# Two result tables for the last two experts, values before powers, and the down products moved inside the next step

## The reference

```
xn  = layernorm(x)
out = x + xn + attention(layernorm(xn) * gamma + beta) @ Wout + moe(xn)
```

```
logits = xn @ Wg.T;  top 2 experts, gates = softmax of the two logits
slot   = running count of the expert in (token, choice) order; kept if slot < 640
h      = rows[slot] @ W1[e];  y = (gelu(h[:, :256]) * h[:, 256:]) @ W2[e]
out[token] += gate * y[slot]    for each kept choice
```

## Time and profile before

| | us |
|---|---|
| median of 3 runs (lowest, highest) | 143.83 (143.49, 144.63) |
| the profiled execution: its own time | 143.37 |
| the profiled execution: span of the records | 141.6 |
| TensorE busy in the span | 108.6 (77%) |
| VectorE busy | 93.5 (66%) |
| ScalarE busy | 68.8 (49%) |
| GpSimd busy | 75.1 (53%) |

### The profile page before, as it was taken

How to read it: one execution, slowest core, us unless ns; L and a number is a source line. 1 busy time by engine, 2 the same in 40 slices (tenths; PEclk the granted TensorE clock), 3 DMA queues, 4 the chain that set the end, 5 groups by cost and what they waited for, 6 DMA issues and landing times.

```text
span 141.6 us, 2294 instructions
## 1 busy us (share of the span) xinstructions
PE 108.6 (77%) x705; PEld 97.6 (69%) x705; DVE 93.5 (66%) x299; ACT 68.8 (49%) x164; POOL 75.1 (53%) x92
## 2 busy tenths in 40 slices
PE   0039999999888884898399999999999988965000
PEld 0029769788777763786298999999999987655000
DVE  0699787696576867897337587897757330463991
ACT  0478773346558751323536666767766644410000
POOL 7700707777787787770000277877877777730000
PEclk9999999999999999999959999999999999999755
DMA  3999999999511111114990011111111111696487
GB/s 98 247 329 287 284 370 326 354 347 300 163 42 59 39 64 54 44 59 108 316 283 8 0 56 37 56 58 39 56 58 58 39 56 56 191 306 187 145 237 219
DMA packets 31980, 21.35 MB, mean 151 GB/s; under 512 B 2224, under 2 KB 29872, under 8 KB 31968
## 3 DMA queue, kind: packets, MB, share of 16 engines
q1 hardware_dynamic: 29104, 16.41, 41.3%
q0 software_dynamic: 2144, 4.53, 9.5%
q10 hardware_dynamic: 720, 0.27, 0.8%
HBM read 10.04 MB, written 11.15 MB: 150 GB/s over the span
## 4 chain that ended last, share of the span: by engine, by line
PE 35%; POOL 22%; DVE 13%; issue 11%; DMA 11%; ACT 2%; SPq 1%; POOLq 1%; DVEq 0%; ACTq 0%
POOL y_rows L447 20%; PE bank_h L935 5%; DMA y_last<-rows,target_i 5%; PE bank_h L937 4%; PE bank_h L936 4%; DMA qT<-y_last 3%; PE bank_x L1105 3%; PE bank_y L1047 3%; DMA xs<-in_x 3%; PE bank_x L1016 3%; PE bank_y L956 2%; PE bank_a L956 2%; POOL y_last L447 2%; DVE pre L763 2%; DVE stats L632 2%
## 5 line engine op out<-in xcount | busy, mean ns | idle before, releaser
L447 POOL DMA_INDIRECT y_rows<-rows,target_i x30 | 30.0, 1000 | 25.6 <-ACT rows L588 17.1
L434 POOL DMA_INDIRECT x_slots<-xa,slot_i x32 | 32.6, 1019 | 14.3 <-issue 9.4
L901 DVE TENSOR_TENSOR hid<-gelu,bank_h 128x384 f32<-128x384 f32 (+2 forms) x32 | 16.3, 510 | 19.2 <-ACT gelu L605 19.1
L1157 PE MATMUL bank_y<-w_sb,hid 128*128 128x128 f32 x172 | 21.9, 276 | 2.3 <-issue 2.3
L1157 PEld LDWEIGHTS bank_y<-w_sb,hid 128*128 128x128 f32 x172 | 21.0, 191 | 2.8 <-issue 2.7
L935 PE MATMUL bank_h<-xg_hi,w_lo 128*128 128x384 f32 (+1 forms) x56 | 20.1, 359 | 1.4 <-DVE xg_lo L852 1.2
L605 ACT ACTIVATE gelu<-bank_h 128x384 f32<-128x384 f32 (+2 forms) x32 | 14.7, 459 | 12.0 <-PE bank_h L937 11.2
L937 PE MATMUL bank_h<-xg_hi,w_hi 128*128 128x384 f32 (+1 forms) x56 | 18.0, 321 | 0.0
L936 PE MATMUL bank_h<-xg_lo,w_hi 128*128 128x384 f32 (+1 forms) x56 | 17.9, 320 | 0.0
L588 ACT ACTIVATE rows<-bank_y,gate_slot 128x128 f32<-128x128 f32 x35 | 10.6, 366 | 10.7 <-PE bank_y L1157 10.7
L935 PEld LDWEIGHTS bank_h<-xg_hi,w_lo 128*128 128x128 f32 x56 | 11.1, 197 | 2.0 <-DVE xg_lo L852 1.6
(11 more groups left out here) (156 smaller groups left out, 241.0 us busy)
## 6 DMA issues: line engine op xcount, KB each, us to landing
x_slots<-vacant SPq DMA_DIRECT2D x7, 340.0 KB, 6.7
rows<-x_slots SPq DMA_DIRECT2D x7, 340.0 KB, 5.7
w_raw<-in_w SPq DMA_DIRECT2D x4, 512.0 KB, 7.3
y_rows<-zeros SPq DMA_DIRECT2D x2, 1024.0 KB, 12.2
expo<-y_rows SPq DMA_DIRECT2D x8, 256.0 KB, 7.3
xs<-in_x SPq DMA_DIRECT2D x4, 256.0 KB, 4.5
y_last<-zeros SPq DMA_DIRECT2D x1, 1024.0 KB, 10.9
qT<-y_last SPq DMA_DIRECT2D x4, 256.0 KB, 3.8
```

Source lines behind the costliest of these rows:

```text
L434: nc.gpsimd.indirect_dma_start(x_slots, bass.IndirectOffsetOnAxis(ap=slot_i[:, k, t:t + 1], axis=0), xa[:, t, :], None,).then_inc(rows_out ...
L447: nc.gpsimd.indirect_dma_start(y_rows if r < R - 1 else y_last, bass.IndirectOffsetOnAxis(ap=target_i[:, n:n + 1], axis=0), rows[:, n, 0:D ...
L901: nc.vector.tensor_tensor(hid[s % 2][:, c, 0:cols], gelu[i % 2][:, 0:cols], bank_h[2 * c + 1][:, 0:cols], ALU.mult).then_inc(hid_ready, 1)
L1157: ins = nc.tensor.matmul(bank_y[:, j * D:(j + 1) * D], hid[s % 2][:, c, j * P:(j + 1) * P], w2_sb[:, e, c, :], start=(c == 0), stop=(c == ...
```

## The change

- Experts 6 and 7 (the last two, `LAST = 2`) get a table each, `y_last[0]` and `y_last[1]`; `y_rows` holds experts 1 to 5. SyncE fills one table more with zeros, waits for 25 scatters before it reads `y_rows`, then for the five of each last table before it reads that one (four transfers each).
- The order of the additions at the end changes: the first choice's four are behind step 14, the dense addition of step 14 and the second choice's four behind step 15, then the four of `y_last[0]`, three of `y_last[1]`, the dense addition of step 15 and the last one.
- `down(s-1)` is issued between the two halves of step s, behind the transposes. `evacuate(s-1)` comes before the gelu of the second half. `y_evac` is raised for each tile, and GpSimd waits tile by tile.
- ScalarE scales the values of a pair of tiles before it takes the pair's power.
- The state of batch 0 is computed by VectorE within the pair loop (at pair 6), that of batch 1 behind the loop; the two states accumulate in two banks.
- In the layer norm VectorE normalises group 1 before the statistics of group 2, and ScalarE copies the first transposes before the third root.
- GpSimd issues one gather of x before the scatters, of which nothing reads the result.

```
@@ note_sum / VectorE, order of the additions
+SUMS_IN_STEP: (14, 1): (("choice", 0),), (15, 1): (("dense", 14), ("choice", 1))
...
+    for g in range(G): note_sum(("last", 0, g), ...)
+    for g in range(G):
+        if g == G - 1:
+            note_dense(S - 1)
+        note_sum(("last", 1, g), ...)
@@ SyncE
             for i in range(2):
-                sp.wait_ge(y_stored[i], 16 * ST * len(range(i, R - 1, 2)))
+                sp.wait_ge(y_stored[i], 16 * ST * len(range(i, R - LAST, 2)))
...
-            sp.wait_ge(y_last_stored, 16 * ST)
+            for i in range(LAST):
+                sp.wait_ge(y_last_stored[i], 16 * ST)
+                for g in range(G):
+                    sp.dma_start(fetched_last[i][:, g * GROUP:(g + 1) * GROUP, :],
+                                 y_last_tiles[i][:, g * GROUP:(g + 1) * GROUP, :]).then_inc(last_in[i][g], 16)
@@ GpSimd
+            nc.gpsimd.indirect_dma_start(
+                unused_rows[:, :], None, x.rearrange("b l d -> (b l) d"),
+                bass.IndirectOffsetOnAxis(ap=partition[:, 0:1], axis=0),
+            ).then_inc(unused_in, 16)
...
-                for i, (j0, nj) in enumerate(PARTS):
-                    pool.wait_ge(y_evac, len(PARTS) * r + i + 1)
-                    for n in range(r * ST + j0, r * ST + j0 + nj):
+                for n in range(r * ST, (r + 1) * ST):
+                    pool.wait_ge(y_evac, n + 1)
@@ ScalarE
             for u in range(U):
+                act.wait_ge(pre_ready, 2 * u + 1)
+                scaled_values(2 * u)
                 act.wait_ge(pre_ready, 2 * u + 2)
+                scaled_values(2 * u + 1)
                 nc.scalar.activation(expo[...], pre[...], ACT.Exp, ...).then_inc(exp_ready, 1)
-                scaled_values(2 * u)
-                scaled_values(2 * u + 1)
...
                         split_rows(s + 1)
-                if s >= 1 and s != first_dense:
-                    evacuate(s - 1)
+                    if c == 0 and s >= 1 and s != first_dense:
+                        evacuate(s - 1)
@@ VectorE
+                if u == STATE_AT:
+                    state_of(0)
             elu(U - 1)
+            state_of(1)
@@ TensorE, up(s)
                     if c == 1 and s + 1 < S and steps[s + 1][3] is not None:
                         transpose_slots(s + 1)
+                    if c == 1 and s >= 1 and s != first_dense:
+                        down(s - 1)
...
                 up(s)
-                if s >= 1 and s != first_dense:
-                    down(s - 1)
```

More of the change, by code:

```diff
@@ L24 @@
 KV_LAG = 4
+STATE_AT = 6
 RESULTS_AT = 2
@@ L30 @@
 LOW_IN_STEP = {(0, 1): 2, (2, 1): 3, (4, 1): 4, (6, 1): 5, (8, 1): 6, (10, 1): 7}
[L31 to L32 removed]
+SUMS_IN_STEP = {(1, 1): (("first", 0),), (2, 1): (("first", 1),), (3, 1): (("first", 2),), (4, 1): (("first", 3),),
+                (5, 1): (("early", 0),), (7, 1): (("early", 1),),
+                (14, 1): (("choice", 0),), (15, 1): (("dense", 14), ("choice", 1))}
 DROPPED = 16384.0
 PARTS = ((0, 3), (3, 2))
+LAST = 2
 TOKEN, RANKS, GATES, ROW = 128, 129, 131, 136
@@ L85, in moe_attention_block, with note_dense @@
             note_sum((kind, u), (2 * u, 2 * u + 1))
+    def note_dense(s):
+        for j in range(GROUP):
+            note_sum(("step", s), (steps[s][1] + j,))
     for s in range(S):
         for c in range(FC):
-            if (s, c) in SUMS_IN_STEP:
-                kind, i = SUMS_IN_STEP[s, c]
+            for kind, i in SUMS_IN_STEP.get((s, c), ()):
                 if kind == "first":
                     note_sum((kind, i), tuple(range(i * GROUP, (i + 1) * GROUP)))
-                else:
+                elif kind == "early":
                     for j in range(GROUP):
                         note_sum((kind, i), (all_token_steps[i][1] + j,))
[L95 to L102, removed]
-    for g in range(G):
-        note_sum(("last", g), tuple(range(g * GROUP, (g + 1) * GROUP)))
+                elif kind == "dense":
+                    note_dense(i)
+                else:
+                    for g in range(G):
+                        note_sum((kind, i, g), tuple(range(g * GROUP, (g + 1) * GROUP)))
+    for g in range(G):
+        note_sum(("last", 0, g), tuple(range(g * GROUP, (g + 1) * GROUP)))
+    for g in range(G):
+        if g == G - 1:
+            note_dense(S - 1)
+        note_sum(("last", 1, g), tuple(range(g * GROUP, (g + 1) * GROUP)))
     def earlier_sum(index, tiles):
@@ L917, in _ @@
                             add_early(n)
-                if s >= 1:
-                    add_dense(s - 1)
-            add_dense(S - 1)
-            for k in range(TOP_K):
-                for g in range(G):
-                    add_rows(("choice", k, g), g, fetched_in[k][g], fetched[:, k, :, :])
-            for g in range(G):
-                add_rows(("last", g), g, last_in[g], fetched_last)
+                        elif kind == "dense":
+                            add_dense(n)
+                        else:
+                            for g in range(G):
+                                add_rows(("choice", n, g), g, fetched_in[n][g], fetched[:, n, :, :])
+            for g in range(G):
+                add_rows(("last", 0, g), g, last_in[0][g], fetched_last[0])
+            for g in range(G):
+                if g == G - 1:
+                    add_dense(S - 1)
+                add_rows(("last", 1, g), g, last_in[1][g], fetched_last[1])
         @block.tensor
```

81 lines of the change are left out of this document (42 added, 39 removed).

## The result

| | before | with the change |
|---|---|---|
| median (12 runs each, side by side) | 143.65 us | 145.0 us |
| lowest, highest | 143.37, 145.91 | 143.65, 147.05 |
| ratio, 95% interval | | 1.0089 (1.0048 to 1.0131) |
| a second comparison on another chip | 145.26 us | 145.44 us, ratio 1.0142 (0.9997 to 1.0286) |

Medians are of all runs, ratios and intervals only of those within 1.5% of their kernel's fastest, so the two can differ. The changed kernel is about 1.3 us slower; 144.8 was forecast. The profiled execution of the changed kernel has a span of 145.3 us, 3.7 more than before. So the traces are compared within, from the first up product of step 2 on. From there to the end of the last addition both profiles of the changed kernel agree within 0.02 us.

What follows compares the result with a forecast made beforehand. TensorE and GpSimd together were taken to bound the expert steps, with a tie of reads and VectorE's additions at the end. Front 0 plus end +1.0, stalls included, on 143.83 gave 144.8 us, range 142.2 to 146.0.

Steps and rivals of the forecast that it cites:

- The total: Whole kernel: +1.0 us, 144.8 by the median, own range 144.2 to 145.6, chance 0.5.
- The front: Values, states, layer norm and gather ahead of the steps: together 0, between -0.5 and +0.4 us.
- Its own signs of being wrong: Among them a first step over 0.5 us away from 70.8, or a second window with a granted clock near 0.5.
- Rival 4: TensorE's clock falls at one of the new stalls, costing about 1.7 us: 146.5 us, chance 0.07.
- The first scatter: GpSimd's first result scatter starts 1.3 us earlier, near 79.0; waits at each expert's first tile use up the lead.
- The stall: TensorE waits for `hid` before `down` behind three-tile halves: 0.38 us five times, 0.6 in step 13, 2.5 us in all.
- The four rows that I added up: Half's end, gelu, `hid` and handover on the way to `down`: 1.43 us, against 1.05 us of other TensorE work.
- The end: VectorE's unbroken 9.5 us of additions behind step 15 ends at 139.4, against 138.40: +1.0 us, with the reads hidden.
- Rival 1: The stall in the steps does not come, TensorE keeps 6.32 us an expert: 142.2 to 142.5 us, chance 0.25.
- The queues: Last scatter beside the reads: served in turns by packet, it would land some 4 us sooner than the 7.00 us measured.

Runs made afterwards that it cites:

- run 8: The change with the down products inside the next step in odd steps only, behind both halves in the others: 143.81 us, 0.999 of the kernel before.
- run 7: The change with the down products inside in step 1 only, and the additions at the end placed earlier: 141.22 us, 0.985 of the kernel before.
- run 5: The change with the down products inside in step 1 and the even steps, behind both halves in odd steps 3 to 13: 144.01 us, 1.002 of before.
- run 6: The change without the four additions of `y_last[0]`, whose scatters and reads stay: 143.46 us, 0.996 of the kernel before.
- run 4: The change with the down products inside in step 1 only, behind both halves in all other steps: 142.22 us, 0.988 of the kernel before.
- run 3: The change with its front undone (value and power order, states, layer norm order, gather): 144.56 us, 1.012 of the kernel before.

## Why the prediction was right, point by point

- **The total.** Forecast +1.0 us, measured +1.3, inside the forecast's own range. The mechanism, a loss in the steps that is larger than the gain at the end, is what the traces show. That the total came so close is in part luck: at the last addition +1.70 were measured for +1.0, and the 0.5 us saved behind it are in no term of the sum, which took the 3.2 us behind it as they were.
- **The front: 0 (-0.5 to +0.4).** Right where it can be read: 6.30 for 6.25 us around the states, and no difference in time when all of it is undone. The start of step 2 itself (80.80 and 79.40 for 78.30) is off by more than the range, but in profiles whose code is the same up to there it lies between 77.22 and 80.80.
- **Its own signs of being wrong.** Two of them came: step 0 started at 72.67 and 71.45 and not within 0.5 us of 70.8, and a second window with the clock at 0.50 was there. By the profiles of the same code neither belongs to the steps that the sum is about; the prediction had no measure of how far the front moves by itself. Rival 4's price of 1.7 us for a low stretch like the one before was too high as well: with it steps 0 and 1 take 7.32 us in run 8, without it 6.35 in run 7.
- **The first scatter, 1.3 us sooner.** Right: 2.01 to 0.70 us behind the start of step 2. Its last one came at 46.65 for 46.4 forecast. But the way there was wrong: I expected a wait at each expert's first tile, and GpSimd waits hardly at all (0.5 us over the usual 0.30 in all). Its lead goes into scatters that take longer, 1.30 to 1.44 us in place of 0.97, one in each of five experts; from first to last it takes 45.95 us, where 34 x 1.27 are 43.2. So the last scatter came where it was forecast by luck. Each of the five long ones starts 0.09 to 0.23 us behind the start of a `w_lo` of VectorE (the first at 85.33, `w_lo` at 85.24). The group of twelve starts near them too, but other kernels speak for `w_lo`: in the kernel before the one scatter that starts so (88.38, `w_lo` at 88.24) takes 1.38, and in run 5 one does (83.65, `w_lo` at 83.58) and takes 1.45, while the group of twelve starts only at 84.59. No run tried it by itself.
- **The stall, 5 x 0.38 + 0.6 = 2.5 us: the size of one was right (0.37 measured, 0.46 in step 13), the sum was too small, 3.03.** Even the one size is right by two errors that cancel. `hid` ends at 85.32 and the group starts at 85.38, 0.06 us behind it and not 0.15; and the first half takes 0.72 us (84.05 to 84.77) and not 0.80. Four experts lose 0.42 to 0.46 us each, the last one, with step 13, 0.71. In these, the group of eight takes 0.85 for 0.81 and the group of twelve, after a wait, 1.36 for 1.26. The expert with step 7 loses 0.57 in another way: no stall on `hid`, but 0.49 us of waiting for `xg_lo`, where before there were 0.25.
- **What causes it: this step named the wrong edit.** I wrote that the group of twelve stalls because it was moved ahead of the second half. Runs 5 and 8 show otherwise: without its move the stall and the whole loss stay (3.00 of 3.03 us), with it the stall goes and 1.41 us of loss stay for the other reasons read off in run 8. What counts for the stall is the group of eight. The four rows that I added up gave the right wait only because the group of eight is missing from "until then TensorE has only the two-tile half and three transposes". I had put it inside the even step and never asked what it had covered. And the same `hid` was not "late by nothing" before: it was 0.44 us early.
- **The end: 139.4 for 138.40.** From step 14 to the last addition's end 18.6 us were forecast, 18.77 measured; the unbroken row of 9.5 us is 133.03 to 142.60, 9.57. That the reads are hidden was right, and run 6 shows by how little.
- **Where the rest comes from.** The end is not at its best either: run 5, in which `down(14)` comes behind the last half of step 15, needs 60.52 - 43.00 = 17.52 us from step 14 on, 1.25 less than the change. With the group inside, the last `hid` ends 9.29 us behind the start of step 14 and not 7.95, and VectorE's row hangs on it. The prediction had this group (1.7 in the sum) but didn't price its alternative.
- **Rival 1 (no stall, 142.2 to 142.5).** It didn't occur, but its price was about right: with the stall taken away, run 4 gives 142.22 us, where the kernel before takes 143.92. (Run 4 takes away the other moves from step 2 on as well.)
- **The queues.** The read that waits for the last scatter is issued at 133.45, 6.0 us behind it, where scatters with no read beside them land after 2.3. The Trainium skill ("DMA: Bandwidth & Descriptors", Queues, rings and completion order) has the queues served in turns, a packet at a time; if the scatter lost only its share by that, it would land nearer to 2.3 us, by our estimate, up to 3.7 us sooner. The trace doesn't agree in size: 6.0 us beside reads, 7.00 before.

Still open: what sets the length of the low stretch of the clock near step 0 (0 to 6.8 us in these profiles), which is worth as much as the effect (up to 1.8 us); whether the change makes the longer one more frequent; and whether `w_lo` is what holds the five long scatters.

## What to carry to other kernels

A group of independent products between two dependent ones is cover, and moving it costs its cover at the old place, whatever it gains at the new one: ask of each moved group first what had been waiting behind it. Read the slack there (0.44 us here) and subtract the length of what goes (0.81). When a wait has been found, its name in the profile is that of the instruction that happened to come next; only moving that instruction alone shows whether it is the cause.

## What the runs showed of the hardware

- Twelve down products after a wait of 0.37 us occupy TensorE for 1.36 us, without one for 1.26 (85.38 to 86.74 in step 3; 99.38 to 100.64 in step 7 of the same profile; the earlier trace rows).
- The granted clock fell behind 2.49 us of an idle TensorE late in the kernel (0.57 in 132.0 to 135.5), and sixteen products took 3.46 us in place of 2.02. A pause of the same 2.49 us stands ahead of the same group in five other profiles (both of the change, runs 3, 6 and 8), where the clock stays at 1.00 and the group takes 2.02; what tells them apart is open.
- A low clock (0.50) for about 6.8 us around steps 0 and 1 lengthens them from 6.35 to 7.96 us (run 7 and run 4, the same code up to there). TensorE idles 0.56 us there in run 7, waiting for `xg_lo`, and not at all in run 4, so the whole stretch grows by less than its products do.
- The last indirect scatter, beside SyncE's reads, lands after 6.0 us (changed) and 7.00 us (before), one with no read beside it after 2.3.
